# A recurrence's tables: readout weights and guard on GpSimd instead of VectorE, and a doubling in three operations

## The chip, the cores and the metric

The kernel runs on one core of one Trainium2 chip. A core has engines that run side by side, each with its own list of instructions: TensorE (matrix products, PE in the rows), VectorE (DVE), ScalarE (ACT), GpSimd (POOL) and SyncE (SP), which here only issues transfers. They wait for each other by counters (semaphores). The metric is the time of one execution on the device in microseconds, the median of several runs.

## The reference

It is a sandwich of three layers over 4096 tokens with 256 features: an expert layer, a linear recurrence over the whole sequence, and the same expert layer again, each added to its input.

```python
x = L0_attn_u                                   # (1, 4096, 256)
x = x + 0.5 * ffn(layernorm(x), Wr, W1, b1, W2, b2)
x = x + ssm(layernorm(x), A_real, A_imag, B, C)
x = x + 0.5 * ffn(layernorm(x), Wr, W1, b1, W2, b2)

# ffn: 8 experts, each token goes to the one of its largest score
probs = softmax(x @ Wr); e = argmax(probs); p = max(probs)
out = p * (gelu(x @ W1[e] + b1[e]) @ W2[e] + b2[e])

# ssm: 128 complex states, real input and output
a = A_real + 1j * A_imag;  denom = 1 - dt / 2 * a
a_disc = (1 + dt / 2 * a) / denom;  B_disc = sqrt(dt) * B / denom[:, None]
h_t = a_disc * h_{t-1} + B_disc @ u_t;  y_t = (C @ h_t).real
```

## The kernel before, in words

**Stages.** Loading, statistics, routing and the splitting of the expert weights into two half-precision parts take the first 85 us. The first expert layer runs to about 306 us, the recurrence (eight chunks of 512 tokens) to about 385, the second expert layer to the end.

**The expert layer.** The tokens are sorted by expert into 39 tiles of at most 128 rows (`NT`). Thirty-two are full; of the seven narrow ones (16 to 112 rows), four (in places 18, 23, 28 and 33 of the order) lie between the full ones and three come last. The loop over tiles `q` is written out by hand for each engine, in a software pipeline:

- GpSimd, per tile: wait for `result(q)` (counter `o`), issue the scatter of the finished rows (line 427), then the two gathers of tile q + 6 (line 421: the rows, and the records with the token's norm and weight).
- ScalarE, per tile: normalise the gathered rows, scale the turned rows to the first half-precision part, and GELU (line 620) in eight pieces of 128 columns.
- TensorE, per tile: turn tile q + 2, first product of tile q + 1 (line 1337, 48 matmuls), second product of tile q (lines 1359 to 1361). The first product of a tile waits for `split_x` of that tile; the second for `split_h`.
- VectorE, per tile: `split_x(q + 2)` (line 1006, the second half-precision part of the input, from PSUM), `split_h(q + 1)` (lines 1018 and 1021, twice: both parts of GELU's result), `result(q)` (lines 1035 and 1038, and in the first layer bn_stats and bn_aggr, lines 1041 and 1042), and in the first layer a piece of table work, `tables_after(q)`.

`result(q)` writes one of two buffers, and so waits for the scatter of tile q - 2 to have landed.

**The tables.** The recurrence is run in a frame that turns with each state, so that a real-valued scan does the work. It needs, for the 512 steps of a chunk, the turns (`turn`: cosine and sine of n times the angle), the readout weights (`back`), a guard that moves weights near zero away from it, and the reciprocal of the product of the two weights. They have 128 x 512 columns in two parts, and are made in pieces after `result(q)`: doublings of `turn` after tiles 2 to 14 (from tile 8 on in pieces of 64 columns), the weights after tiles 15 to 22 (two instructions each on 128 columns), the guard after tiles 23 to 30 (three instructions each on 128 columns), product and reciprocal of 64 columns after tiles 31 to 37, and a last piece with the rest of the tables after the loop. `link` makes an engine wait for its own instruction's end.

After the layer SyncE waits for all scatters, reloads x (eight transfers), GpSimd computes the norm's factors of the first chunk, and VectorE goes on in `turn_by_rates` (line 1174).

## Time and profile before

| what | value |
|---|---|
| median of 3 runs | 613.46 us (611.41 to 613.84) |
| profiled execution | 611.62 us, of which the span from first to last instruction is 609.8 |
| TensorE busy | 550.4 us (90% of the span) |
| VectorE busy | 479.6 us (79%) |
| ScalarE busy | 410.0 us (67%) |
| GpSimd busy | 287.5 us (47%) |
| granted TensorE clock, mean | 0.987 |

Busy time is that of an engine's own instructions, and a share of the whole span is an average over the stages. Starts are microseconds from the start of the span. What an engine waited for is inferred from the counters' events. Matmuls overlap, and their ends are modelled. An operation of GpSimd counts from when it begins to read to when its writes are done, so what it waits for within it is in its duration.

### The profile page before, as it was taken

The page shows a single profiled execution, that of the slowest core. Times are in us where ns is not written, and L with a number is a line of the kernel's source. Part 1 is how long each engine was busy: PE and PEld are TensorE (multiplying, and loading weights), DVE is VectorE, ACT ScalarE, POOL GpSimd, SP SyncE. Part 2 cuts the span into 40 slices and gives each one's busy share as a digit, 9 for nine tenths or more (in the row PEclk, how much of TensorE's full clock was granted, in tenths as well). Part 3 has the DMA queues.
Part 4 walks back from the last instruction along what each step waited for, and adds up shares of the span by engine and source line. Part 5 has one row for each costly group of instructions (what it writes and reads, how often), then busy time and mean ns, then how long its engine had stood idle before and what let it go on. Part 6 is the DMA issues. An engine that isn't in the chain of part 4 may idle for free.

```text
span 609.8 us, 18742 instructions
## 1 busy us (share of the span) xinstructions
PE 550.4 (90%) x6518; PEld 505.6 (83%) x6518; DVE 479.6 (79%) x1082; ACT 410.0 (67%) x966; POOL 287.5 (47%) x325
## 2 busy tenths in 40 slices
PE   5993148999999999999989998699999999999996
PEld 5993047999998999998976776599999999999996
DVE  5778997999999889898978988466667666666674
ACT  3888978767766676766615862386766777766763
POOL 0024165565454555654136243556555555545532
PEclk9999999999999999999999996899999999999999
DMA  7999102111121111111053223212111111111110
GB/s 248 369 370 378 38 26 97 54 55 46 46 53 47 37 53 45 53 38 45 23 191 125 75 99 107 60 44 57 47 45 53 54 48 44 46 46 46 52 28 16
DMA packets 34874, 51.95 MB, mean 85 GB/s; under 512 B 6747, under 2 KB 27933, under 8 KB 34528
## 3 DMA queue, kind: packets, MB, share of 16 engines
q1 hardware_dynamic: 24800, 31.93, 15.3%
q0 software_dynamic: 9984, 18.83, 11.3%
q8 instruction: 56, 0.92, 0.6%
q14 instruction: 34, 0.28, 0.2%
HBM read 37.98 MB, written 14.59 MB: 86 GB/s over the span
## 4 chain that ended last, share of the span: by engine, by line
PE 71%; DVE 10%; issue 6%; POOL 4%; DMA 3%; ACT 3%; DVEq 1%; SPq 0%; ACTq 0%; POOLq 0%
PE banks L1337 27%; PE banks L1359 10%; PE banks L1361 9%; PE banks L1360 9%; PE banks L1267 4%; PE banks L1312 2%; PE banks L1239 2%; PE banks L1446 2%; DVE weights_arena L1018 2%; DVE weights_arena L1021 1%; PE banks L1414 1%; PE banks L1429 1%; POOL weights_arena L421 1%; DMA recf<-records,sorti 1%; DVE weights_arena L1038 1%
## 5 line engine op out<-in xcount | busy, mean ns | idle before, releaser
L620 ACT ACTIVATE weights_arena<-banks,b1t,inv 128x128 f32<-128x128 f32 (+7 forms) x624 | 220.6, 459 | 34.4 <-PE banks L1337 34.3
L1337 PE MATMUL banks<-weights_arena 128*128 128x128 f16 (+7 forms) x3744 | 207.0, 214 | 3.0 <-DVE weights_arena L1006 2.2
L1337 PEld LDWEIGHTS banks<-weights_arena 128*128 x3744 | 199.3, 98 | 6.6 <-issue 5.5
L1359 PE MATMUL banks<-weights_arena 128*128 (+7 forms) x624 | 170.2, 273 | 0.5 <-DVE weights_arena L1021 0.3
L1361 PE MATMUL banks<-weights_arena 128*128 (+7 forms) x624 | 170.1, 273 | 0.0
L1360 PE MATMUL banks<-weights_arena 128*128 (+7 forms) x624 | 170.1, 273 | 0.0
L1018 DVE TENSOR_SCALAR weights_arena<-weights_arena,hscale 128x512 f16<-128x512 f32 (+5 forms) x156 | 74.7, 479 | 57.1 <-ACT weights_arena L620 56.2
L1021 DVE SCALAR_TENSOR_TENSOR weights_arena<-weights_arena,hscale 128x512 f16<-128x512 f32 (+5 forms) x156 | 109.8, 704 | 5.6
L601 ACT ACTIVATE weights_arena<-banks,xscale 128x256 f16<-128x256 f32 (+7 forms) x78 | 35.7, 457 | 89.8 <-PE banks L1312 89.8
L421 POOL DMA_INDIRECT recf<-records,sorti x78 | 76.5, 981 | 24.6 <-issue 23.5
L427 POOL DMA_INDIRECT x_after_ffn<-weights_arena,sorti x39 | 39.7, 1019 | 80.8 <-DVE weights_arena L1042 74.2
L427 POOL DMA_INDIRECT out<-weights_arena,sorti x39 | 39.5, 1013 | 78.2 <-DVE weights_arena L1038 70.8
L1359 PEld LDWEIGHTS banks<-weights_arena 128*128 128x128 f16 (+7 forms) x624 | 62.3, 100 | 7.3 <-issue 1.1
L1361 PEld LDWEIGHTS banks<-weights_arena 128*128 128x128 f16 (+7 forms) x624 | 62.4, 100 | 6.4
L1360 PEld LDWEIGHTS banks<-weights_arena 128*128 128x128 f16 (+7 forms) x624 | 62.4, 100 | 5.6
L421 POOL DMA_INDIRECT weights_arena<-L_attn_u,sorti x39 | 45.7, 1171 | 29.0 <-DVE sorti L984 17.4
L585 ACT ACTIVATE weights_arena<-weights_arena,recf 128x256 f32<-128x256 f32 (+7 forms) x78 | 46.1, 591 | 9.6 <-DMA recf<-records,sorti 9.5
L1035 DVE SCALAR_TENSOR_TENSOR weights_arena<-banks,inv,weights_arena 128x256 f32<-128x256 f32 (+7 forms) x78 | 37.7, 483 | 14.3 <-issue 5.6
L421 POOL DMA_INDIRECT weights_arena<-x_after_ssm,sorti x39 | 40.5, 1038 | 15.1 <-issue 11.6
L1006 DVE SCALAR_TENSOR_TENSOR weights_arena<-banks,xscale,weights_arena 128x256 f16<-128x256 f32 (+7 forms) x78 | 35.6, 457 | 12.5 <-ACT weights_arena L601 7.8
L1038 DVE SCALAR_TENSOR_TENSOR weights_arena<-weights_arena,recf 128x256 f32<-128x256 f32 (+7 forms) x78 | 37.8, 484 | 2.8
L729 DVE SCALAR_TENSOR_TENSOR weights_arena<-weights_arena,wscale 128x2048 f16<-128x2048 f32 x16 | 37.2, 2342 | 2.7 <-ACT weights_arena L516 2.7
(238 smaller groups left out, 648.7 us busy)
## 6 DMA issues: line engine op xcount, KB each, us to landing
weights_arena<-L_ffn_W SPq DMA_DIRECT2D x16, 1024.0 KB, 12.6
weights_arena<-x_after_ffn SPq DMA_DIRECT2D x8, 516.0 KB, 7.3
weights_arena<-L_attn_u SPq DMA_DIRECT2D x8, 512.0 KB, 11.1
x_after_ssm<-weights_arena SPq DMA_DIRECT2D x8, 512.0 KB, 2.9
weights_arena<-L_ffn_b SPq DMA_DIRECT2D x2, 1024.0 KB, 5.2
recf<-records,sorti POOLq DMA_INDIRECT x78, 2.5
weights_arena<-L_attn_u,sorti POOLq DMA_INDIRECT x39, 3.2
x_after_ffn<-weights_arena,sorti POOLq DMA_INDIRECT x39, 2.5
```

The lines of the kernel that those rows point to most:

```text
L421: pool.indirect_dma_start(to, None, source, bass.IndirectOffsetOnAxis(ap=sorti[:, slot(q), index:index + 1].bitcast(U32), axis=0)).then_in ...
L427: pool.indirect_dma_start(dst, bass.IndirectOffsetOnAxis(ap=sorti[:, slot(q), 2:3].bitcast(U32), axis=0), og[q % 2] if ph == 1 else og[q % ...
L585: act.activation(xng[q % 2][0:w], xg[q % RING][0:w], ACT.Identity, bias=recf[0:w, q % RING, 0:1], scale=recf[0:w, q % RING, 1:2]).then_inc ...
L620: last = act.activation(hb[q % 2][:, f, 0:width(q)], src, ACT.Gelu, bias=b1t[:, bass.ds(e * FC + f, 1)], scale=inv1[:, bass.ds(e, 1)])
L1018: dve.tensor_scalar(hs[q % 2][:, 0, f, of], hb[q % 2][:, f, of], sc, None, ALU.mult) \
L1021: dve.scalar_tensor_tensor(hs[q % 2][:, 1, f, of], hb[q % 2][:, f, of], sc, hs[q % 2][:, 0, f, of], ALU.mult, ALU.subtract).then_inc(s["hs ...
L1035: dve.scalar_tensor_tensor(o, acc, i2, b2b[0:w, bass.ds(e * D, D)], ALU.mult, ALU.add) \
L1038: last = dve.scalar_tensor_tensor(o, o, recf[0:w, q % RING, 2:3], xg[q % RING][0:w], ALU.mult, ALU.add)
L1337: last = pe.matmul(acc[:, f * P:f * P + n_cols], weights[wpart * DC + d], xts[q % 2][:, xpart, d, 0:n_cols], start=(n == 0), stop=(n == 5))
L1359: pe.matmul(acc, hs[q % 2][:, 0, f, of], high, start=(f == 0), stop=False)
L1360: pe.matmul(acc, hs[q % 2][:, 0, f, of], low, start=False, stop=False)
L1361: last = pe.matmul(acc, hs[q % 2][:, 1, f, of], high, start=False, stop=(f == FC - 1))
```

## The change

Readout weights, guard and the product of the weights leave VectorE. GpSimd makes them in 13 operations on 128 x 512 columns each (`weights_after`), one behind the scatter and the two gathers of each of tiles 15 to 27; the guard and the weights are taken apart into operations with two inputs or with one input and scalars. A counter tells GpSimd that the turns are made (`turns_made`, at tile 14), another tells VectorE that the product is (`weights_made`); VectorE waits for it from tile 29 on, and keeps only the reciprocals, all eight within the loop (tiles 29 to 36). A doubling takes three instructions in place of four: the two products with the sine are one instruction over both parts. Four counters of the start are merged into two (`pool_made`, `dve_made`).

```diff
--- before.py
+++ after.py
@@ -375,15 +375,15 @@
...
-            pool.wait_ge(iota_done, 3)
-            pool.wait_ge(rho_in, 1)
-            pool.tensor_tensor(ev[:, 13:14], ev[:, 12:13], mhalf[:, 0:1], ALU.pow).then_inc(rho_out, 1)
+            pool.wait_ge(pool_made, 3)
+            pool.wait_ge(dve_made, 3)
+            pool.tensor_tensor(ev[:, 13:14], ev[:, 12:13], mhalf[:, 0:1], ALU.pow).then_inc(pool_made, 1)
@@ -401,6 +401,34 @@
                 chain.link(pool.tensor_scalar(vid[:, NJ:NTE], over_experts[:, NJ:NTE, 0], -1.0, None, ALU.add))
                 pool.tensor_scalar(vid_h, vid, BIG / P, None, ALU.add).then_inc(S[ph]["vids"], 1)
 
+            def weights_after(q):
+
+                link = chain.link
+                if q == 15:
+                    pool.wait_ge(turns_made, 1)
+                    link(pool.tensor_scalar(aa[:, 0, :], turn[:, 0, :], ev[:, 15:16], None, ALU.mult))
+                elif q == 16:
+                    link(pool.tensor_scalar(aa[:, 1, :], turn[:, 1, :], ev[:, 15:16], None, ALU.mult))
+                elif q == 17:
+                    link(pool.tensor_scalar(inverse[:, 0, :], turn[:, 0, :], ev[:, 14:15], None, ALU.mult))
+                elif q == 18:
+                    link(pool.tensor_scalar(inverse[:, 1, :], turn[:, 1, :], ev[:, 14:15], None, ALU.mult))
+                elif q == 19:
+                    link(pool.tensor_tensor(back[:, 0, :], inverse[:, 0, :], aa[:, 1, :], ALU.subtract))
+                elif q == 20:
+                    link(pool.tensor_tensor(back[:, 1, :], inverse[:, 1, :], aa[:, 0, :], ALU.add))
+                elif q in (21, 22):
+                    weight = back[:, q - 21, :]
+                    link(pool.tensor_tensor(aa[:, q - 21, :], weight, weight, ALU.mult))
+                elif q in (23, 24):
+                    near = aa[:, q - 23, :]
+                    link(pool.tensor_scalar(near, near, NEAR_ZERO ** 2, STAND_IN, ALU.is_lt, ALU.mult))
+                elif q in (25, 26):
+                    weight = back[:, q - 25, :]
+                    link(pool.tensor_tensor(weight, weight, aa[:, q - 25, :], ALU.add))
+                elif q == 27:
+                    pool.tensor_tensor(aa[:, 0, :], back[:, 0, :], back[:, 1, :], ALU.mult).then_inc(weights_made, 1)
+
             def ffn(ph, src, dst):
                 s = S[ph]
                 table = src
@@ -434,6 +462,8 @@
                     scatter(q)
                     if q + RING < NT:
                         fetch(q + RING)
+                    if ph == 1:
+                        weights_after(q)
 
             tile_slots(1)
             ffn(1, u, x1_dram)
@@ -681,15 +711,15 @@
...
-            dve.tensor_scalar(ident[:], iota_r[:], part[:], None, ALU.is_equal).then_inc(const_done, 1)
+            dve.tensor_scalar(ident[:], iota_r[:], part[:], None, ALU.is_equal).then_inc(dve_made, 1)
@@ -764,9 +794,9 @@
-                dve.scalar_tensor_tensor(col(12), col(11), col(11), col(16), ALU.mult, ALU.add).then_inc(rho_in, 1)
-                dve.wait_ge(rho_in, 1)
-                dve.wait_ge(rho_out, 1)
+                dve.scalar_tensor_tensor(col(12), col(11), col(11), col(16), ALU.mult, ALU.add).then_inc(dve_made, 1)
+                dve.wait_ge(dve_made, 3)
+                dve.wait_ge(pool_made, 5)
@@ -774,33 +804,15 @@
             def double(n, begin=0, end=None):
 
                 end = n if end is None else end
-                c0, s0 = turn[:, 0, begin:end], turn[:, 1, begin:end]
+                of, to = slice(begin, end), slice(n + begin, n + end)
                 cn, sn = turn[:, 0, n - 1:n], turn[:, 1, n - 1:n]
-                dve.tensor_scalar(back[:, 0, begin:end], s0, sn, None, ALU.mult)
-                link(dve.tensor_scalar(back[:, 1, begin:end], c0, sn, None, ALU.mult))
-                dve.scalar_tensor_tensor(turn[:, 0, n + begin:n + end], c0, cn, back[:, 0, begin:end], ALU.mult, ALU.subtract)
-                link(dve.scalar_tensor_tensor(turn[:, 1, n + begin:n + end], s0, cn, back[:, 1, begin:end], ALU.mult, ALU.add))
-
-            def readout(part, begin, end):
+                link(dve.tensor_scalar(back[:, :, of], turn[:, :, of], sn, None, ALU.mult))
+                dve.scalar_tensor_tensor(turn[:, 0, to], turn[:, 0, of], cn, back[:, 1, of], ALU.mult, ALU.subtract)
+                link(dve.scalar_tensor_tensor(turn[:, 1, to], turn[:, 1, of], cn, back[:, 0, of], ALU.mult, ALU.add))
+
+            def inverse_of_both(begin, end):
 
                 of = slice(begin, end)
-                col_a, col_b, how = (0, 1, ALU.subtract) if part == 0 else (1, 0, ALU.add)
-                tmp = aa[:, part, of]
-                link(dve.tensor_scalar(tmp, turn[:, col_b, of], col(15), None, ALU.mult))
-                link(dve.scalar_tensor_tensor(back[:, part, of], turn[:, col_a, of], col(14), tmp, ALU.mult, how))
-
-            def away_from_zero(part, begin, end):
-
-                of = slice(begin, end)
-                tmp, weight = aa[:, part, of], back[:, part, of]
-                link(dve.tensor_tensor(tmp, weight, weight, ALU.mult))
-                link(dve.tensor_scalar(tmp, tmp, NEAR_ZERO ** 2, None, ALU.is_lt))
-                link(dve.scalar_tensor_tensor(weight, tmp, STAND_IN, weight, ALU.mult, ALU.add))
-
-            def inverse_of_both(begin, end):
-
-                of = slice(begin, end)
-                link(dve.tensor_tensor(aa[:, 0, of], back[:, 0, of], back[:, 1, of], ALU.mult))
                 link(dve.reciprocal(aa[:, 0, of], aa[:, 0, of]))
 
             def inverses(part):
@@ -826,7 +838,6 @@
-                piece = CH // 4 * ((q - 15) // 2)
@@ -835,13 +846,11 @@
                     double(CH // 4, CH // 8 * (q - 9), CH // 8 * (q - 8))
                 elif 11 <= q < 15:
                     double(CH // 2, CH // 8 * (q - 11), CH // 8 * (q - 10))
-                elif 15 <= q < 23:
-                    readout((q - 15) % 2, piece, piece + CH // 4)
-                elif 23 <= q < 31:
-                    piece = CH // 4 * ((q - 23) // 2)
-                    away_from_zero((q - 23) % 2, piece, piece + CH // 4)
-                elif 31 <= q < NT - 1:
-                    inverse_of_both(CH // 8 * (q - 31), CH // 8 * (q - 30))
+                    if q == 14:
+                        dve.sem_inc(turns_made, 1)
+                elif 29 <= q < 37:
+                    dve.wait_ge(weights_made, 1)
+                    inverse_of_both(CH // 8 * (q - 29), CH // 8 * (q - 28))
 
             def bounds_up():
 
@@ -1065,7 +1074,6 @@
                 if ph == 1:
                     dve.memset(state[:], 0.0)
                     dve.memset(all_ones, 1.0)
-                    inverse_of_both(CH // 8 * (NT - 32), CH)
                     inverses(0)
                     inverses(1)
                     carries()
```

## Rows read from the trace of the kernel before

**Rows 1.** Busy time by stretch, first expert layer: length; PE, PEld, DVE, ACT, POOL busy.

```profile
168.38:191.70 23.32, 22.59 (x299) 20.78 (x297) 21.44 (x52) 15.39 (x40) 11.46 (x12) 1.00 0.18 47
191.70:272.67 80.97, 80.35 (x1111) 75.12 (x1111) 72.32 (x175) 56.10 (x150) 46.68 (x47) 1.00 0.18 46
272.67:293.95 21.28, 20.73 (x299) 18.90 (x296) 19.03 (x46) 14.52 (x40) 9.95 (x10) 1.00 0.17 46
```

**Rows 2.** Busy time by stretch, second expert layer.

```profile
470.72:492.72 22.00, 22.00 (x298) 20.91 (x296) 15.12 (x29) 15.38 (x40) 12.07 (x13) 1.00 0.18 51
492.72:572.72 80.00, 80.00 (x1113) 75.24 (x1111) 54.37 (x106) 56.05 (x150) 45.16 (x46) 1.00 0.18 47
572.72:593.27 20.55, 20.55 (x299) 18.94 (x296) 14.12 (x29) 14.53 (x40) 8.33 (x9) 1.00 0.16 39
```

**Rows 3.** Waits of TensorE, 157.35 to 293.95: total us, times, longest.

```profile
PE banks L1337 <- DVE weights_arena L1006: 1.2, 2, 0.6
```

**Rows 4.** Timeline of VectorE at both layers' ends: start, length, line, [idle before].

```profile
305.96 0.47 DVE L1035 SCALAR_TENSOR_TENSOR weights_arena<-banks,inv,weights_arena 16x256 f32<-16x256 f32 x1 [0.38 <-PE banks L1361]
...
313.57 0.21 DVE L825 TENSOR_SCALAR back<-back,rho 128x1 f32<-128x1 f32 x1
315.83 0.31 DVE L1174 TENSOR_SCALAR weights_arena<-ident,rs 128x128 f32<-128x128 f32 x1 [2.05 <-POOL sd L449]
...
604.84 0.47 DVE L1035 SCALAR_TENSOR_TENSOR weights_arena<-banks,inv,weights_arena 16x256 f32<-16x256 f32 x1 [1.72 <-PE banks L1361]
```

**Rows 5.** Timeline of VectorE, a tile with a 64-wide doubling.

```profile
160.37 0.18 DVE L1042 BATCH_NORM_AGGREGATE weights_arena<-stats 128x2 f32<-128x6 f32 x1
160.47 0.22 DVE L779 TENSOR_SCALAR back<-turn 128x64 f32<-128x64 f32 x1
160.60 0.25 DVE L780 TENSOR_SCALAR back<-turn 128x64 f32<-128x64 f32 x1
...
161.91 0.72 DVE L1018 TENSOR_SCALAR weights_arena<-weights_arena,hscale 128x512 f16<-128x512 f32 x1
```

**Rows 6.** Groups of VectorE by line, 104 to 316 us: busy, mean ns, idle before.

```profile
L804 DVE RECIPROCAL weights_arena<-weights_arena 128x64 f32<-128x64 f32 x8 | 4.4, 553 | 0.3
...
L790 DVE SCALAR_TENSOR_TENSOR back<-turn,ev,weights_arena 128x128 f32<-128x128 f32 x8 | 2.8, 352 | 0.3
...
L789 DVE TENSOR_SCALAR weights_arena<-turn,ev 128x128 f32<-128x128 f32 x8 | 2.0, 254 | 0.0
```

**Rows 7.** Timeline of GpSimd, transfers of the same tile.

```profile
161.37 1.01 POOL L427 DMA_INDIRECT x_after_ffn<-weights_arena,sorti  x1 [2.38 <-DVE weights_arena L1042]
...
163.96 0.94 POOL L421 DMA_INDIRECT recf<-records,sorti  x1 [0.30 <-issue]
```

**Rows 8.** Timeline of VectorE, a tile with a 32-wide doubling.

```profile
144.48 0.48 DVE L1018 TENSOR_SCALAR weights_arena<-weights_arena,hscale 128x512 f16<-128x512 f32 x1
```

**Rows 9.** Timeline of VectorE, tiles without table work.

```profile
105.15 0.48 DVE L1035 SCALAR_TENSOR_TENSOR weights_arena<-banks,inv,weights_arena 128x256 f32<-128x256 f32 x1
...
106.65 0.18 DVE L1042 BATCH_NORM_AGGREGATE weights_arena<-stats 128x2 f32<-128x6 f32 x1
...
107.16 0.48 DVE L1018 TENSOR_SCALAR weights_arena<-weights_arena,hscale 128x512 f16<-128x512 f32 x1
...
109.80 0.48 DVE L1035 SCALAR_TENSOR_TENSOR weights_arena<-banks,inv,weights_arena 128x256 f32<-128x256 f32 x1
```

**Rows 10.** Groups by line and shape of GpSimd, 54 to 64 us.

```profile
L398 POOL TENSOR_TENSOR weights_arena<-weights_arena 128x160 f32<-128x160 f32 x1 | 0.5, 523 | 0.1
L398 POOL TENSOR_TENSOR weights_arena<-weights_arena 128x80 f32<-128x80 f32 x1 | 0.3, 323 | 0.1
```

**Rows 11.** Timeline of VectorE and GpSimd at 60 us.

```profile
60.10 2.33 DVE L729 SCALAR_TENSOR_TENSOR weights_arena<-weights_arena,wscale 128x2048 f16<-128x2048 f32 x1
...
60.27 2.33 POOL L402 TENSOR_SCALAR weights_arena<-weights_arena 128x40 f16<-128x40 f32 x1
```

**Rows 12.** DMA issues of the first layer's scatter: median us to landing.

```profile
x_after_ffn<-weights_arena,sorti POOLq DMA_INDIRECT x39, 2.5
```

22 lines of the change are left out of this document (11 added, 11 removed).

## The prediction

> **What bounds the kernel now.** I set the two expert layers beside each other, because they run the same tiles over the same expert weights and only the first carries the table work on VectorE. Cut at the starts of the same first products (tiles 12, 14, 18, 33 and 37), the view of busy time by stretch gives, for tiles 14 to 18, 18 to 33 and 33 to 37, lengths of 23.32, 80.97 and 21.28 us in the first layer [rows 1] and 22.00, 80.00 and 20.55 in the second [rows 2]. In the second layer TensorE is busy for the whole of each. In the first it is idle for part of each, and VectorE is busy for 21.44 of 23.32, 72.32 of 80.97 and 19.03 of 21.28. So TensorE bounds the second layer and VectorE, at these places, the first; the list of waits names `split_x` (line 1006) as what the first product waited for [rows 3]. The differences, 1.32 + 0.97 + 0.73 = 3.02 us, are what VectorE costs between tiles 14 and 37. From the start of tile 37's first product to the last tile's `result` it is 305.96 - 293.95 = 12.01 in the first layer and 604.84 - 593.27 = 11.57 in the second [rows 1, 2, 4]: 0.44 more. **3.46 us is the ceiling** of what relief of VectorE can bring here.
>
> Behind the layer nothing else catches the end: VectorE's own tail of table work ends at 313.57 + 0.21 = 313.78, and its next work starts at 315.83 [rows 4], having waited for GpSimd, which waited for the reload of x. That cover is 2.05 us. The last scatter, the reload and all that follows hang on the last `result`, so an earlier end of the layer is passed on whole; the tail loses one small piece of work itself (line 803 and 804 for the last 64 columns), under cover.
>
> **The change, part by part.**
>
> *Doublings in three operations (tiles 2 to 14).* Before, lines 779 and 780 start at 160.47 and 160.60, so the first costs 0.13 us of VectorE's time, and from line 1042 to line 1018 it takes 161.91 - 160.37 = 1.54 [rows 5]. The new first instruction works on 2 x 64 columns at once. No row has that form; the nearest are 128 x 64 at 0.25 (line 780) [rows 5] and 128 x 128 at 0.254 (line 789) [rows 6]. So it costs nothing to 0.05 more than line 780, and I take 0.03: a saving of 0.10 a tile, 1.3 over 13 tiles. There is a second effect. Line 1018 took 0.72 while a scatter was issued (161.37 to 162.38) [rows 5, 7] and 0.48 in the tile with half as wide a doubling [rows 8]; starting 0.10 earlier it may get ahead of it, which is worth 0 to 0.24 a tile. A tile without tables takes VectorE 109.80 - 105.15 = 4.65 us, of which 0.51 lies between lines 1042 and 1018 [rows 9]; TensorE takes 22.00 / 4 = 5.50 [rows 2]. With a 64-wide doubling VectorE needs 4.65 + (1.54 - 0.51) + 0.24 = 5.92, 0.42 too much for each of seven tiles (8 to 14), 2.9 in all; 1.32 of it reached TensorE, so a lead of some 1.6 took up the rest. With 0.10 less a tile 7 x 0.32 = 2.2 stands against a lead of 1.6 + 0.6 (tiles 2 to 7) = 2.2; with 0.34 less, 0.6. I take 0.2 as left over: **1.1 us gained of 1.32**.
>
> *Weights, guard and product leave VectorE (tiles 15 to 30).* The weights were two instructions a tile (0.254 and 0.352 us [rows 6]), the guard three, the product one before each reciprocal. Now tiles 15 to 28 have no table work, VectorE needs 4.65 of 5.50, and its lead grows by up to 0.85 a tile. Tiles 29 to 36 keep the reciprocal at 0.553 [rows 6], so 5.3 of 5.50. The narrow tiles (18, 23, 28 and 33), where TensorE takes some 0.8 less (15 x 5.50 - 80.00 = 2.5 for three of them [rows 2]) and VectorE still runs `result` at full length, were what VectorE paid for in the last two stretches; a lead of 2 us covers each. **0.9 of 0.97, 0.7 of 0.73, 0.4 of 0.44.**
>
> *Thirteen GpSimd operations, one behind each tile's transfers (tiles 15 to 27).* What GpSimd does for a tile now runs from 161.37 to 163.96 + 0.94 = 164.90, 3.53 us [rows 7]. No row shows 128 x 512 on GpSimd. The largest is 128 x 160 with two inputs at 523 ns, and 128 x 80 took 323 [rows 10]: 2.5 ns a column, so 0.523 + 352 x 0.0025 = 1.40 us. The bounds are 0.52 (no dearer than the smaller one) and 1.67 (in proportion). For the forms with one input and a scalar, the only row of any width is 40 columns in 2.33 us, and that one began at 60.27, right behind a VectorE instruction that began at 60.10 and took 2.33, and ended 0.17 after it [rows 11]: a wait, not work. I give them the same 1.40. Then a tile is 3.53 + 0.30 + 1.40 = 5.23 of 5.50: it fits, with little over. Queued behind each operation (the link waits for its end) are the next scatter and two gathers. The gathers are issued six tiles ahead. A scatter starts 161.37 - 160.55 = 0.82 after `result` ends [rows 5, 7] and lands 2.5 later [rows 12]; `result` of two tiles later waits for it, 1.7 (106.65 + 0.18 - 105.15 [rows 9]) before that tile's own end, so the slack is 11.0 - 1.7 - 0.82 - 2.5 = 6.0 us. The work is hidden as long as GpSimd runs less than that behind. At tile 29 VectorE waits for the last of it, issued at tile 27: a tile and more of slack.
>
> *Semaphores.* The merged counters are waited on in the same order by the same engines; two new waits replace two old ones. Nothing is queued that was not before: zero.
>
> *Does GpSimd hold up VectorE?* GpSimd waits there for a two-input VectorE instruction [rows 11], and line 1018 at 0.72 instead of 0.48 [rows 5, 8] shows the reverse. When VectorE has its lead, the operation starts 0.3 after the second gather, 164.90 + 0.30 - 160.55 = 4.65 after a `result` ends, which with a period of 5.50 is 0.5 before the next `result`'s bn_stats: mostly over work that reads PSUM or a single input. A collision is then paid from an idle 0.85 a tile. I take nothing, with a bound of 1.40 a tile. The Trainium skill, SBUF — State Buffer, section Who interferes with whom, says that a VectorE instruction with two SBUF inputs contends with a GpSimd one that reads SBUF, and that the later one is blocked for the whole of the earlier; the wait of 2.33 us agrees, and by that rule the reverse could cost whole operations, which is the first rival below.
>
> **Sum.** 1.1 + 0.9 + 0.7 + 0.4 = 3.1 us off the profiled execution's 611.62, so 608.5. The median of the runs is 1.84 above that execution (613.46), so the predicted median is 613.46 - 3.1 = **610.4**. 0.5% is 3.07 us, about what this measurement can tell from no change: the forecast lies on that line.
>
> **Rivals.**
> - *The port takes half of it back.* If each operation holds VectorE for about half its length, 0.7 a tile, VectorE needs 5.35 of 5.50 in tiles 15 to 27: no loss on wide tiles, but no lead for the narrow ones, so the 0.9 is not gained and 0.1 of the rest goes: 613.46 - 2.1 = 611.4. For the whole 1.40, 6.05 of 5.50 costs 13 x 0.55 = 7.2 less a lead of some 2, 5.2 in place of the 0.97, and the time is 613.46 - 2.2 + 4.2 = 615.5. For it: the two rows above. Against it: of the lines of a tile only 1021 and 1038 read two SBUF tensors, and only 1018 is slowed in the rows; together they are about half of VectorE's time.
> - *Slower: GpSimd becomes the bound.* If an operation takes d, GpSimd runs 3.83 + d a tile; above d = 1.67 it falls behind, and above 1.67 + 6.0 / 13 = 2.1 the scatters come too late for `result`, which stalls. At d = 3.0 that is 13 x 1.33 - 6.0 = 11.3 us: 613.46 - 3.1 + 11.3 = 621.7. For it: the instruction of 40 columns that took 2.33 [rows 11]. Against it: the slope of the two rows that waited for nothing [rows 10].
> - *The change does not do what it says.* The lead does not build because GpSimd and VectorE fall into step (5.23 and 4.65 plus what they cost each other), and the doublings' collision with the scatter stays at 0.72: only some 0.7 comes from the doublings: 612.8.
>
> **Numbers.** Forecast 0.62 (between a gain of 2.5 and the ceiling: 610.0 to 611.0); half taken back 0.20; no effect 0.10; GpSimd the bound 0.08. The line of 0.5% cuts the forecast's own range, and the runs of one kernel spread by 0.4%, so of 0.62 about 0.43 falls under 3.07 us faster, the rest and the second and third cases within 0.5%, and 0.09 above. The range reaches from the lowest run less the ceiling, 611.41 - 3.46 = 608.0, to 613.3, which takes in the two cases without much gain and leaves out the whole-length lock and the GpSimd bound.
>
> **What would show it.** Right: the first layer's stretches near 22.0, 80.0 and 20.6; TensorE busy throughout; line 789 to 798 gone from VectorE; the new GpSimd rows at 0.5 to 1.7 us; the first wait of line 1018 for GELU instead of none. The doubling's saving shows as the distance from line 1042 to line 1018 at 1.2 to 1.45 instead of 1.54. Wrong: GpSimd rows over 2 us, scatters later and later from tile 15 to 27, `result` waiting for a scatter; or lines 1018, 1021 and 1038 stretched to over 1 us in those tiles.

## The result, and the profile after

The changed kernel took 615.66 us in the median of 20 runs (613.41 to 617.39), the kernel before 611.85 in 20 runs beside it (609.21 to 615.65): a ratio of 1.0066, 95% interval 1.0050 to 1.0081. It is slower: the whole interval lies at 0.5% or more. 610.4 in a range of 608.0 to 613.3 was forecast. Of all the runs below, one execution stood far apart (`e3_pow`: 701.45 us at a mean granted clock of 0.77, the others at 0.92 and more) and is left out there.

Busy time by stretch of the changed kernel, first expert layer, cut at the first products of tiles 14, 18, 33 and 37 (answers to [rows 1]; after the length come the busy times of PE, PEld, DVE, ACT and POOL):

```profile
166.84:188.83 21.99, 21.99 (x298) 20.91 (x296) 19.96 (x46) 15.38 (x40) 12.08 (x13) 1.00 0.19 48
188.83:274.64 85.81, 81.95 (x1112) 74.73 (x1110) 74.12 (x136) 55.32 (x150) 65.78 (x58) 1.00 0.16 42
274.64:296.33 21.69, 20.73 (x299) 18.90 (x296) 19.25 (x43) 14.57 (x40) 10.33 (x11) 1.00 0.19 45
```

Tiles 14 to 18 gained the whole 1.32 us, but tiles 18 to 33, forecast at 80.1, took 85.81 against 80.97. Finer cuts put the loss at tiles 23 to 28 (28.59 us, before 26.72) and 28 to 33 (30.43, before 26.69); tiles 18 to 23 stand at 26.78. The last result comes at

```profile
307.91 0.47 DVE L1044 SCALAR_TENSOR_TENSOR weights_arena<-banks,inv,weights_arena 16x256 f32<-16x256 f32 x1 [0.36 <-PE banks L1369]
```

so the end takes 307.91 - 296.33 = 11.58 against 12.01 [rows 1, 4]. From tile 14 to this result it is 141.07 us, where it was 305.96 - 168.38 = 137.58: **3.49 us lost in the place where 3.1 were to be gained**. Of the rest of the span, 1.5 us were gained up to tile 14, 0.5 lost between the layers and 0.7 at the start of the second layer. The first and the last are within what executions of the same code differ by: the changed kernel and three of the kernels below whose code is the same there (the late wait, the held and the later products) reach tile 14 between 166.84 and 169.23 us, and take 214.4 to 215.4 us from the second layer's first product to the end.

What did go as forecast: a tile with a 64-wide doubling, on VectorE (answers to [rows 5]; L1027 is the former L1018):

```profile
158.11 0.18 DVE L1051 BATCH_NORM_AGGREGATE weights_arena<-stats 128x2 f32<-128x6 f32 x1
158.21 0.25 DVE L809 TENSOR_SCALAR back<-turn 128x128 f32<-128x128 f32 x1
...
159.52 0.48 DVE L1027 TENSOR_SCALAR weights_arena<-weights_arena,hscale 128x512 f16<-128x512 f32 x1
```

The distance is 1.41 in place of 1.54, and line 1027 is back at 0.48 from 0.72. It does not get ahead of the scatter for that; the scatter of this tile is

```profile
159.10 1.01 POOL L455 DMA_INDIRECT x_after_ffn<-weights_arena,sorti  x1 [2.09 <-DVE weights_arena L1051]
```

and line 1027 starts 0.42 into it, where line 1018 had started 161.91 - 161.37 = 0.54 into it [rows 5, 7]. In the profiles of before, after and the doublings alone (125 to 186 us, 512 columns) this line took 0.47 to 0.49 wherever it started up to 0.45 into a scatter, and 0.72 in all seven places where it started 0.54 or 0.55 into one.

What did not go as forecast, first on GpSimd, from one scatter to the next with an operation between them (answers to [rows 7]):

```profile
186.92 1.13 POOL L455 DMA_INDIRECT x_after_ffn<-weights_arena,sorti  x1 [2.37 <-DVE weights_arena L1051]
188.35 0.97 POOL L449 DMA_INDIRECT weights_arena<-L_attn_u,sorti  x1 [0.30 <-issue]
189.63 0.95 POOL L449 DMA_INDIRECT recf<-records,sorti  x1 [0.31 <-issue]
190.63 1.79 POOL L409 TENSOR_SCALAR weights_arena<-turn,ev 128x512 f32<-128x512 f32 x1
193.23 1.17 POOL L455 DMA_INDIRECT x_after_ffn<-weights_arena,sorti  x1 [0.82 <-POOL weights_arena L409]
```

One round (from one scatter to the next) takes 193.23 - 186.92 = 6.31 us; TensorE needs 5.50 a tile. The operation took 1.79, and the scatter behind it began only 0.82 after its end. GpSimd's groups by line, 160 to 297 us, show two prices:

```profile
L425 POOL TENSOR_SCALAR weights_arena<-weights_arena 128x512 f32<-128x512 f32 x2 | 4.3, 2142 | 0.2
L428 POOL TENSOR_TENSOR back<-back,weights_arena 128x512 f32<-128x512 f32 x2 | 2.5, 1272 | 0.1
```

The six operations with one input took 1.78 to 2.27 us, the seven with two 1.05 to 1.28. The rounds take 6.3 to 6.7 us with one input and 5.4 to 5.9 with two. So GpSimd falls behind from tile 15 on, and everything in its queue with it. The waits of ScalarE and of TensorE, 155 to 297 us (total, times, longest; before, ScalarE waited for no transfer there, and TensorE's row is [rows 3]):

```profile
ACT weights_arena L615 <- DMA recf<-records,sorti: 22.8, 11, 3.8
```

```profile
PE banks L1345 <- DVE weights_arena L1015: 3.2, 5, 1.0
PE banks L1367 <- DVE weights_arena L1030: 0.6, 1, 0.6
```

Line 615 is ScalarE's norm, which needs the gathered rows of three tiles ahead; it stands in ScalarE's order ahead of the next tile's GELU (line 650). The chain at 237 us, on ScalarE and then on VectorE:

```profile
236.87 0.60 ACT L615 ACTIVATE weights_arena<-weights_arena,recf 48x256 f32<-48x256 f32 x1 [3.77 <-DMA recf<-records,sorti]
237.38 2.86 ACT L650 ACTIVATE weights_arena<-banks,b1t,inv 128x128 f32<-128x128 f32 x8
```

```profile
239.05 0.49 DVE L1027 TENSOR_SCALAR weights_arena<-weights_arena,hscale 128x512 f16<-128x512 f32 x1 [1.78 <-ACT weights_arena L650]
```

A late gather, a late norm, a late GELU, an idle VectorE, and with it the lead is gone. The second thing that differs is the length of VectorE's own instructions when GpSimd runs an operation beside them:

```profile
227.61 2.02 DVE L1030 SCALAR_TENSOR_TENSOR weights_arena<-weights_arena,hscale 128x512 f16<-128x512 f32 x1
```

```profile
228.02 1.05 POOL L422 TENSOR_TENSOR weights_arena<-back 128x512 f32<-128x512 f32 x1
```

Line 1030 reads two SBUF tensors and takes 0.75 alone; here, and at four other places between 221 and 264 us, it took 1.97 to 2.25. Two theories stood: the **queue** (GpSimd's longer round delays gathers and scatters) and the **port** (GpSimd's reads hold VectorE).

### The profile page after: what moved, and what is told of

Read it like the earlier page. It is cut to its first block, busy times and chain, and to the rows that moved or that the text cites. A ratio compares the mean times of both kernels' runs of the same rounds, so it can differ in the third digit from the quotient of the medians.

```text
span 613.0 us, 18692 instructions
## 1 busy us (share of the span) xinstructions
PE 549.0 (90%) x6518; PEld 503.4 (82%) x6518; DVE 477.3 (78%) x1021; ACT 408.8 (67%) x966; POOL 310.6 (51%) x338
## 4 chain that ended last, share of the span: by engine, by line
PE 62%; DVE 9%; POOL 8%; issue 7%; DMA 7%; SPq 3%; ACT 2%; DVEq 0%; ACTq 0%; POOLq 0%
PE banks L1345 25%; PE banks L1367 9%; PE banks L1369 9%; PE banks L1368 9%; DMA recf<-records,sorti 2%; PE banks L1320 2%; POOL weights_arena L449 2%; DMA weights_arena<-L_attn_u 2%; PE banks L1275 2%; DVE weights_arena L1030 1%; SPq L327 1%; PE banks L1422 1%; SPq L310 1%; PE banks L1437 1%; POOL recf L449 1%
## 5 line engine op out<-in xcount | busy, mean ns | idle before, releaser
L1027 DVE TENSOR_SCALAR weights_arena<-weights_arena,hscale 128x512 f16<-128x512 f32 (+5 forms) x156 | 74.6, 478 | 64.0 <-ACT weights_arena L650 63.4
L1030 DVE SCALAR_TENSOR_TENSOR weights_arena<-weights_arena,hscale 128x512 f16<-128x512 f32 (+5 forms) x156 | 118.0, 756 | 5.6
L449 POOL DMA_INDIRECT recf<-records,sorti x78 | 78.9, 1011 | 24.9 <-issue 23.5
L1047 DVE SCALAR_TENSOR_TENSOR weights_arena<-weights_arena,recf 128x256 f32<-128x256 f32 (+7 forms) x78 | 40.3, 516 | 2.8
```

Of the source, the lines that this page charges most:

```text
L449: pool.indirect_dma_start(to, None, source, bass.IndirectOffsetOnAxis(ap=sorti[:, slot(q), index:index + 1].bitcast(U32), axis=0)).then_in ...
L1027: dve.tensor_scalar(hs[q % 2][:, 0, f, of], hb[q % 2][:, f, of], sc, None, ALU.mult) \
L1030: dve.scalar_tensor_tensor(hs[q % 2][:, 1, f, of], hb[q % 2][:, f, of], sc, hs[q % 2][:, 0, f, of], ALU.mult, ALU.subtract).then_inc(s["hs ...
L1047: last = dve.scalar_tensor_tensor(o, o, recf[0:w, q % RING, 2:3], xg[q % RING][0:w], ALU.mult, ALU.add)
```

## The experiments

In all of them "stretches" are the lengths of tiles 14 to 18, 18 to 23, 23 to 28, 28 to 33, 33 to 37 and the end, from the same cuts. Before they are 23.31, 27.57, 26.72, 26.69, 21.28 and 12.01; after 22.00, 26.78, 28.59, 30.43, 21.69 and 11.58. Ratios are to the kernel before, run beside each on the same chip; runs without a ratio had one execution.

**Doublings alone** (`e1_doublings`): the kernel before with the three-operation `double`; weights, guard and product stay on VectorE.

```diff
-                dve.tensor_scalar(back[:, 0, begin:end], s0, sn, None, ALU.mult)
-                link(dve.tensor_scalar(back[:, 1, begin:end], c0, sn, None, ALU.mult))
+                link(dve.tensor_scalar(back[:, :, of], turn[:, :, of], sn, None, ALU.mult))
...
```

> Only the doublings in three operations; weights, guard and product stay on VectorE in their pieces. Queue theory (GpSimd's tile became longer than TensorE's, gathers come late) and port theory (GpSimd's operations hold VectorE's two-input instructions) both put the whole loss on the GpSimd operations: then this is 1.3 to 1.8 us faster than before, first-layer stretches 14 to 18 at 22.0 to 22.2 and 18 to 33 at 80.5 to 81. If the loss came from the doublings or from the rest of the change, it is 1 us or more slower.

Measured: 610.94 us, ratio 0.9998 (0.9972 to 1.0024); stretches 22.00, 26.78, 26.72, 27.02, 21.29, 12.37. The layer is 1.41 us shorter (2.10 gained in tiles 14 to 23, 0.70 lost again from 28 on), and the total does not show it (below, "where the gain went").

**Nothing on GpSimd** (`e2_no_gpsimd`): the changed kernel without its 13 operations; VectorE makes the weights behind the loop, and its reciprocals in tiles 29 to 36 work on other numbers, so that its load in the loop stays.

```diff
-                    if ph == 1:
-                        weights_after(q)
...
...
+                    for part_of in range(2):
+                        readout(part_of, 0, CH)
+                    for part_of in range(2):
+                        away_from_zero(part_of, 0, CH)
+                    link(dve.tensor_tensor(aa[:, 0, :], back[:, 0, :], back[:, 1, :], ALU.mult))
+                    inverse_of_both(0, CH)
                     inverses(0)
```

> The changed kernel with no weights, guard or product in the loop, neither on GpSimd nor on VectorE: VectorE makes them in full width after the loop, and within it takes reciprocals of other numbers of the same size, which are not used. Both theories: first-layer stretches as in the second layer, 22.0, 80.0 and 20.6, and no wait of ScalarE's norm for a gather; the time as a whole is some 5 us above before, as 11 us of VectorE's work now lie behind the layer, of which 2 are covered. If the loss had another cause than the GpSimd operations, stretches 18 to 33 stay at 85 and 33 to 37 at 21.7.

Measured: 616.65, ratio 1.0105 (1.0053 to 1.0157), since the work behind the loop adds 97.17 - 89.59 = 7.6 us between the layers; stretches 22.00, 26.78, 26.72, 26.49, 20.76, 11.98. Without GpSimd's operations the layer's loss is gone whole: they are its cause, not the order of VectorE's remaining work. (The waits on the two new counters go with them; in the changed kernel neither engine stood idle at one, and the next run has neither and loses as much.)

**A queue without a port** (`e3_pow`): as the last, but behind each of tiles 15 to 27 GpSimd raises 7 columns to a power, with the same wait behind it; that reads nearly nothing.

```diff
+                if 15 <= q < 28:
+                    link(pool.tensor_tensor(var1[:, 0:7], iota_r[:, 1:8], mhalf[:, 0:7], ALU.pow))
```

> As the one before, with 13 GpSimd operations in the same places that read only 7 columns (a power, estimated at 1.5 us from 8 columns in 1.66 and 4 in 1.04), so that GpSimd is as long as in the changed kernel but reads next to nothing. Queue theory: stretch 18 to 33 at 83 or more, ScalarE's norm waits 10 us or more for gathers. Port theory: 80.0 to 80.5, and the second instruction of split_h stays at 0.75.

Measured: 623.65 (three executions), ratio 1.0223 (1.0159 to 1.0287); stretches 22.00, 26.78, 27.27, 31.34, 22.69, 11.58. GpSimd, then ScalarE's wait:

```profile
208.81 1.64 POOL L408 TENSOR_TENSOR var<-iota_r,mhalf 128x7 f32<-128x7 f32 x1
211.28 1.04 POOL L433 DMA_INDIRECT x_after_ffn<-weights_arena,sorti  x1 [0.83 <-POOL var L408]
```

```profile
ACT weights_arena L593 <- DMA recf<-records,sorti: 23.6, 11, 3.4
```

The powers take 1.56 us in the mean and the next scatter again waits 0.83: rounds of 6.0 to 6.2 us, 79.6 for all 13, where those of the real operations took 78.7. VectorE's two-input lines stand at their means of before (0.70 and 0.48 us, 186 to 275 us), so the port has no part. That alone costs as much in the layer (141.68 us from tile 14 to the last result, after 141.07) as the real operations do. The queue is sufficient.

**More gathers ahead** (`e4_ring8`): the changed kernel with `RING = 8` for 6, two more buffers of gathered rows; the reload shares the counters of the first load to make room.

```diff
-RING = 6
+RING = 8
...
```

> The changed kernel with gathers eight tiles ahead instead of six (and the reload's counters shared with the first load's, to have counters for it). Queue theory: gathers are in time again, stretch 18 to 33 back to 80.0 to 80.8, time 2.5 to 3.4 us below before. Port theory: the stretch stays over 83, the time 1 us or more above before. If both act, in between: 81 to 83.

Measured: 614.55, ratio 1.0064 (1.0038 to 1.0090); stretches 22.00, 26.78, 26.72, 31.24, 21.57, 11.57. The norm waits for no gather any more, but the rounds are as long as in the changed kernel, and now the scatters are too late. VectorE's waits, 225 to 280 us, and two rows of its timeline:

```profile
DVE weights_arena L1044 <- DMA x_after_ffn<-weights_arena,sorti: 5.9, 3, 3.4
```

```profile
251.88 0.48 DVE L1044 SCALAR_TENSOR_TENSOR weights_arena<-banks,inv,weights_arena 128x256 f32<-128x256 f32 x1 [3.41 <-DMA x_after_ffn<-weights_arena,sorti]
252.40 1.49 DVE L1047 SCALAR_TENSOR_TENSOR weights_arena<-weights_arena,recf 128x256 f32<-128x256 f32 x1
```

`result` may not overwrite its buffer until the scatter of two tiles earlier has landed. One late transfer took the place of another: the backlog, not the depth, is the trouble. Line 1047 at 1.49 for 0.48 shows the port beside it: it took 1.05 in the mean of 15 tiles (186 to 275 us), so this run does not part the two.

**The late wait** (`e5_deferred`): the changed kernel with one thing moved. GpSimd waits for an operation's end just before its next operation, no longer right behind it, so that the scatter between does not wait.

```diff
-                link = chain.link
+                def link(instruction):
+                    instruction.then_inc(pool_chain, 1)
+                    chain.n += 1
+                if 15 < q < 28:
+                    pool.wait_ge(pool_chain, chain.n)
```

> The changed kernel, but GpSimd waits for an operation of the weights just before the next one, not right behind it, so the scatter can follow in 0.3 us and not in 0.82. Queue theory (GpSimd's own 6.3 to 6.6 us a tile against TensorE's 5.5 delay scatters and gathers): a tile with a two-input operation falls to about 5.4 and one with a one-input operation to about 6.1, so tiles 23 to 28 take about 27.0 us and 28 to 33 about 27.0, where the changed kernel's profile has 28.59 and 30.43, and the time is 611 to 613. Port theory (a two-input operation of GpSimd holds VectorE's two-input operations from 0.75 to 2.0 us): the stretches stay 1 to 2 us longer than those of the kernel before, 18 to 33 in all about 84, and the time is 614 to 616.

Measured: 610.94, ratio 0.9985 (0.9953 to 1.0016); stretches 22.00, 26.78, 26.72, 26.50, 20.77, 11.58. GpSimd, and busy time from tile 18 to 28 in two stretches:

```profile
192.29 1.79 POOL L415 TENSOR_SCALAR weights_arena<-turn,ev 128x512 f32<-128x512 f32 x1
194.26 1.05 POOL L461 DMA_INDIRECT x_after_ffn<-weights_arena,sorti  x1 [0.18 <-issue]
```

```profile
190.50:217.28 26.78, 26.78 (x372) 25.43 (x370) 22.45 (x46) 18.82 (x50) 22.66 (x21) 1.00 0.17 44
217.28:244.00 26.72, 26.72 (x373) 25.07 (x370) 22.12 (x46) 18.67 (x50) 22.39 (x21) 1.00 0.18 46
```

The scatter follows after 0.18 us in place of 0.82; the operations are the same and take as long. TensorE is busy throughout, and the layer is 134.35 us from tile 14 to the last result: 6.72 less than after, 3.23 less than before. **The 0.64 us of hand-over (from an operation's end to the next transfer), behind 12 of the 13 operations, decided the sign of the layer's change.** The whole time is below the changed kernel's (the intervals are apart) and can't be told from that of before. With another timing the operations also held VectorE less (line 1036 took 0.69 us in the mean of 186 to 275 us, its counterpart 1030 in the changed kernel 0.97); that the loss needs no port is shown by the powers, not by this run.

**Late wait and more gathers** (`e6_both`): both edits.

```diff
-RING = 6
+RING = 8
...
+                if 15 < q < 28:
+                    pool.wait_ge(pool_chain, chain.n)
```

> The late wait and eight gathers ahead in place of six. Queue theory: nothing waits for a gather or a scatter any longer, tiles 23 to 28 take 26.7 us and 28 to 33 at most 26.8, and the time is 610 to 611. Port theory: as with the late wait alone, 28 to 33 at 28 to 30 and the time 613 to 615.

Measured: 610.66, ratio 0.9993 (0.9963 to 1.0022); stretches 22.00, 26.78, 27.75, 27.33, 21.24, 11.59. No one waits for a transfer, yet the layer is 2.3 us longer than with the late wait alone: TensorE waited 2.0 us for `split_x` (line 1021 of this kernel), and line 1053 (the former 1047) took 0.735 us in the mean of 186 to 275 us for 0.510 there. That is the port.

**Port against queue at one load** (`e9_two_inputs`, `e10_pow_deferred`): both edits, and in place of the weights equal operations that take GpSimd alike: 13 two-input products of 128x512 (1.28 us) in the one, 12 powers of 5 columns (1.26 us) in the other, which has none behind tile 27. The weights are made by VectorE behind the loop, as above.

```diff
+                if 15 <= q < 27:
+                    link(pool.tensor_tensor(aa[:, 0, :], turn[:, 0, :], turn[:, 1, :], ALU.mult))
...
+                    link(pool.tensor_tensor(var1[:, 0:5], iota_r[:, 1:6], mhalf[:, 0:5], ALU.pow))
```

> Late wait, eight gathers ahead, and in place of the weights 13 equal two-input operations of 128x512 behind tiles 15 to 27 (the weights are made by VectorE behind the loop, which adds some 7 us there). Port with no queue: 1.28 us each keeps GpSimd at 5.4 us a tile. Queue theory: tiles 18 to 23, 23 to 28 and 28 to 33 stand at 26.8, 26.7 and 26.5 us. Port theory: each operation takes 1.2 to 1.5 us from VectorE, which has about 0.5 us free in a tile, so each of the stretches 18 to 23 and 23 to 28 is 2 to 4 us longer.

> The same, but with 13 powers over 5 columns, which take about as long on GpSimd (1.1 to 1.3 us) and read nearly nothing (the weights are made by VectorE behind the loop). Queue with no port. Both theories: GpSimd at 5.4 us a tile keeps up, and the three stretches stand at 26.8, 26.7 and 26.5 us. If they are longer than that, GpSimd's time in the queue costs even under 5.5 us a tile, and the two-input kernel's stretches must be read against this one's.

Measured, one execution each: 617.0 and 619.39. Stretches of the products: 22.00, 27.69, 26.72, 26.49, 20.55, 11.58; of the powers: 22.00, 26.78, 26.72, 26.49, 20.77, 11.58. VectorE's groups by line, 186 to 275 us, with the products and then with the powers:

```profile
L1051 DVE SCALAR_TENSOR_TENSOR weights_arena<-weights_arena,recf 128x256 f32<-128x256 f32 (+3 forms) x16 | 12.6, 790 | 0.6
```

```profile
L1051 DVE SCALAR_TENSOR_TENSOR weights_arena<-weights_arena,recf 128x256 f32<-128x256 f32 (+3 forms) x17 | 8.2, 484 | 0.6
```

Over 16 tiles line 1051 lost 16 x 0.306 = 4.9 us and line 1031 (0.628 for 0.489) about 4.7, and of these 9.6 us only 0.9 reached TensorE: VectorE had the lead to pay it. The port theory's 2 to 4 us a stretch are refuted for this place of the operations; the powers show that rounds of 5.0 to 5.7 us cost nothing.

**The last products held back** (`e12_held_inverses`): the late wait, and VectorE begins its two products behind the last tile when GpSimd says that the last scatter has been issued. The reason for it, a longer last scatter, is told in the next section ("so an earlier end of the layer is passed on whole").

```diff
+                if ph == 1:
+                    pool.sem_inc(weights_made, 1)
...
+                    dve.wait_ge(weights_made, 2)
                     inverses(0)
```

> The kernel with the late wait, and VectorE begins the two products behind the last tile (L820 in the changed kernel) only when GpSimd has issued the last scatter. In the changed kernel and the three built on it the last scatter took 1.49 us while such a product ran on VectorE at its start, in the kernel before 0.98, and the reload of the rows began 5.14 to 5.22 us behind the last result in place of 4.63. Theory that VectorE's two-input operation holds the scatter: the scatter is back at 0.98 and the reload at 4.6, the stage between the layers is 0.5 us shorter, and the time about 608 to 610. Rival, that the late start has another cause (the last tile's own landing, or GpSimd's queue): the reload stays at 5.1 to 5.2. In both the first layer's stretches stay at 22.00, 26.78, 26.72, 26.50, 20.77 and 11.58.

Measured: 610.28, ratio 0.9996 (0.9969 to 1.0023); stretches 22.00, 26.78, 26.72, 27.66, 21.22, 11.58. The signal overtook the scatter: VectorE's product began 0.17 us ahead of it instead of 0.70, and the scatter took

```profile
305.37 1.37 POOL L461 DMA_INDIRECT x_after_ffn<-weights_arena,sorti  x1 [0.97 <-DVE weights_arena L1059]
```

with the reload at 5.02. So this run did not take the product away from the scatter's start; the next one did. It told something else: up to tile 37 its loop is that of the late wait alone, and yet 28 to 33 and 33 to 37 took 1.6 us more, with TensorE waiting 1.5 us for `split_x`. The port's price changes from one execution to another, with where GpSimd's operation falls in VectorE's tile: here `result` of one narrow tile was held for 2.04 us (line 1055, for 0.48) beside an operation of 1.05.

**The last products later** (`e14_later_products`): the late wait, with the last two pieces of the reciprocals moved behind the last tile, ahead of the two products.

```diff
-                elif 29 <= q < 37:
+                elif 29 <= q < 35:
...
+                    inverse_of_both(CH // 8 * 6, CH // 8 * 7)
+                    inverse_of_both(CH // 8 * 7, CH)
                     inverses(0)
```

> The late wait, and the last two pieces of 64 reciprocals are made behind the last tile, ahead of the two products, in place of tiles 35 and 36: some 1.2 us more work of one input on VectorE there. So the first product begins about 0.5 us behind the last scatter's start and not 0.7 ahead of it. Theory that a two-input operation of VectorE at the scatter's start lengthens it: the last scatter takes 0.98 us in place of 1.49 and the reload begins 4.6 us behind the last result in place of 5.2, though VectorE has more to do there. Rival, that the longer scatter comes from GpSimd's operations in the loop or from the shorter end: 1.4 to 1.5 and 5.1 to 5.2 as before. The end, 11.58, gains nothing or loses up to 0.4 by neither.

Measured, one execution: 612.74; stretches 22.00, 26.78, 26.72, 26.50, 21.07, 11.58. The last scatter on GpSimd, and VectorE's first product:

```profile
306.30 0.97 POOL L461 DMA_INDIRECT x_after_ffn<-weights_arena,sorti  x1 [1.03 <-DVE weights_arena L1057]
```

```profile
306.71 1.42 DVE L826 TENSOR_TENSOR weights_arena<-back,weights_arena 128x512 f32<-128x512 f32 x2
```

The reload begins 4.79 us behind the last result, 0.43 earlier than with the late wait alone, though VectorE has more to do behind the last tile. The theory held for the scatter: with the product starting 0.41 us behind its start it takes 0.97, with one running at its start 1.49. For the reload 4.6 was forecast.

**ScalarE in place of GpSimd** (`e13_scalar_held`): the doublings in three operations; no table work on GpSimd. ScalarE makes four operations of 512 columns, VectorE the rest, with the last products held as in `e12_held_inverses`.

```diff
+                    if ph == 1 and q in (16, 17):
+                        act.wait_ge(turns_made, 1)
+                        act.activation(aa[:, q - 16, :], turn[:, 17 - q, :], ACT.Copy, scale=ev[:, 15:16]).then_inc(weights_made, 1)
+                    if ph == 1 and q in (21, 23):
+                        part = (q - 21) // 2
+                        act.wait_ge(turns_made, part + 2)
+                        act.activation(aa[:, part, :], back[:, part, :], ACT.Square).then_inc(weights_made, 1)
...
```

> ScalarE in place of GpSimd: it makes the two multiplications by the readout's small part behind its norm of tiles 19 and 20 and the two squares behind those of 24 and 26; VectorE makes the weights with one operation of 256 columns in each of four tiles, tests the squares and adds in pieces of 128 in eight tiles, and the product and reciprocals in pieces of 64 in tiles 30 to 37; the last products are held as in the other kernel of this call. If the work itself was never the trouble but only where it was put (GpSimd's queue and port), the stretches stand at 22.00, 26.78, 26.72, 26.6, 20.9 and 11.6 and the time is that of the other kernel, 608 to 610. If ScalarE's longest wait, for TensorE, is no room (its GELU and norm come late), the stretches of 18 to 28 are 0.5 to 1 us longer.

Measured: **609.40, ratio 0.9963 (0.9942 to 0.9984)**; stretches 22.00, 26.78, 26.72, 26.50, 20.67, 12.05. ScalarE's groups by line, 160 to 297 us:

```profile
L631 ACT ACTIVATE weights_arena<-turn,ev 128x512 f32<-128x512 f32 x2 | 1.4, 711 | 0.0
L635 ACT ACTIVATE weights_arena<-back 128x512 f32<-128x512 f32 x2 | 1.2, 617 | 0.0
```

Four operations of 0.6 to 0.7 us, once in a tile at most, on an engine that waited 31 us for TensorE in these tiles, and TensorE waits for nobody. Its interval lies below 1, and below the changed kernel's.

**The same without the hold** (`e15_scalar_later`; the edit is against the run above): the last 64 columns of product and reciprocal stand behind the last tile, as in the kernel before.

```diff
-                elif 30 <= q < NT - 1:
+                elif 30 <= q < NT - 2:
...
-                    dve.wait_ge(weights_made, 5)
+                    inverse_of_both(CH // 8 * 7, CH)
                     inverses(0)
```

> ScalarE in place of GpSimd, without the hold; the last piece of product and reciprocals (64 columns) stands behind the last tile, as in the kernel before, so VectorE's products begin 0.07 us behind the last scatter's start. Theory that they hold the scatter only when they run at its start: the scatter takes 0.98 and the reload begins at 4.63, 0.4 earlier than with the hold (5.04); the time is 608.5 to 609.5, or that of the kernel with the hold, 609.4, if the clock of the chunks covers it. Rival: the scatter stays at 1.4 and the reload at 5.0. The stretches stand at 22.00, 26.78, 26.72, 26.50, 20.7 and 11.6 to 12.05 in both.

Measured: **609.50, ratio 0.9976 (0.9954 to 0.9999)**; stretches 22.00, 26.78, 26.72, 26.50, 20.66, 12.00; last scatter 0.98 us, reload at 4.64 as forecast. So a second kernel with this work on ScalarE is faster than before, if only just by its interval; whether it or the one with the hold is the better can't be told.

## Why the prediction was wrong

*Doublings: right.* 1.1 of 1.32 us was forecast for tiles 14 to 18; all of it came, in the changed kernel and with the doublings alone. The 0.24 a tile of line 1018 came too, though not as the prediction had it: the line starts 0.42 into the scatter in place of 0.54 and is not slowed there, without getting ahead of it.

*Weights, guard and product leave VectorE: right in size, where GpSimd does not spoil it.* 0.9, 0.7 and 0.4 were forecast; with the late wait 26.78 + 26.72 + 26.50 = 80.00 for 80.97, 20.77 for 21.28 and 11.58 for 12.01 give 0.97, 0.51 and 0.43. With the doublings that is 3.23 against a sum of 3.1 and a ceiling of 3.46.

*"Then a tile is 3.53 + 0.30 + 1.40 = 5.23 of 5.50: it fits": this step failed, in two of its terms.* The 1.40 was 1.05 to 1.28 for two inputs, but 1.78 to 2.27 for one, of which the prediction said "I give them the same 1.40", over a row of 40 columns in 2.33 us that it had put down to a wait. That reading was right, but the trace of before had more: the same line runs again at 380.87 us and takes 0.71 there (into float16), where line 398 with two inputs takes 0.26 for 40 columns. And the 0.30 is the gap between two transfers, which wait for nothing. Behind an operation that GpSimd itself waits for, the gap is 0.82; the prediction had that number, for the way from `result` to its scatter, and did not use it for GpSimd's wait on itself, though it wrote that "the link waits for its end". So a round was 6.3 to 6.7 us with one input and 5.4 to 5.9 with two. The powers show that rounds of 6.0 to 6.2 are enough for the whole loss, the late wait that 0.64 us less is enough to lose nothing: the one-input operations at their real price still make rounds of 5.5 to 6.1 us there, which costs the lead a little and TensorE nothing.

*"The gathers are issued six tiles ahead" was taken for ample.* The slack that was worked out, 6.0 us, is the scatter's. Before, the gather of tile 12 is issued, and its norm starts, at

```profile
141.40 0.94 POOL L421 DMA_INDIRECT recf<-records,sorti  x1 [0.30 <-issue]
```

```profile
146.98 0.59 ACT L585 ACTIVATE weights_arena<-weights_arena,recf 128x256 f32<-128x256 f32 x1
```

With 2.3 us to landing (its median in 120 to 200 us), counted from the issue's start or its end, that leaves 2.3 to 3.3 us, which three or four rounds of 0.8 too much use up. The norm is early by three tiles, and a gather waits for `result` of six tiles earlier. With eight ahead this wait went, and the scatter's 6.0 us were used up in its turn.

*The rivals.* "GpSimd becomes the bound", at 0.08, is what happened: its mechanism, scatters and gathers too late, and its place. Its threshold, d above 1.67, left out the hand-over; with 0.82 for 0.30 it is 1.15, which all but two of the 13 operations pass. "The port takes half of it back" happened too, between 0 and 2.3 us as the phase falls, but it was not needed for the loss. The Trainium skill, SBUF — State Buffer, section Who interferes with whom, says that a VectorE instruction with two SBUF inputs contends with a GpSimd one that reads SBUF, and that the ports they share are an exclusive lock. The trace agrees in size: line 1030 took 2.02 us for 0.75 beside an operation of 1.05. By the records line 1030 had started 0.41 us ahead of the operation and was held all the same, so which of the two is held can't be read from their starts. That the rival's price for whole operations, 615.5, stands next to the measured 615.66 is luck: it put the loss on the port, and the powers lose as much without one. "I take nothing" stood on a timing of GpSimd's operation that held only while GpSimd was on time, and that was misread: before, a `result` that ends at 106.83 runs its two-input line 1038 from 105.67 to 106.15 and bn_stats from 106.19, so 4.65 after the `result` ahead of it, at a period of 5.50, is 0.2 before bn_stats and not 0.5, within line 1038. It is this line that was held with both edits and with the products.

*"so an earlier end of the layer is passed on whole": not so.* Where the gain went with the late wait: 3.23 us shorter in the layer, and in the profiled execution 2.39 longer from the last `result` to the second layer's first product (91.98 for 89.59). Its parts, by the first table product of each of the scan's chunks: to the first 14.11 for 13.16 behind the last result; from there to the second 7.03 for 6.09, where VectorE waited 2.5 us for the reload of its rows (before 1.5); from the third to the fourth 7.49 for 6.17; the rest 0.82 less. That from third to fourth, beside the same one after, with the granted clock third from the end:

```profile
329.88:337.37 7.49, 7.26 (x30) 5.44 (x31) 5.96 (x10) 5.01 (x14) 1.40 (x6) 0.77 0.20 70
```

```profile
333.89:340.06 6.17, 6.17 (x38) 4.90 (x37) 5.89 (x10) 3.55 (x9) 1.40 (x6) 1.00 0.25 85
```

For part of it TensorE ran at 1.2 GHz, after the second chunk's step, in which it was busy for 4.93 of 7.03 us, and another of 5.80 in 5.89. Of the kernels that make the weights within the layer, the profiles of seven show such a stretch somewhere between 16 and 33 us behind the last `result` (the doublings alone, eight gathers ahead, the late wait, the held and the later products, both with ScalarE), those of before, after and of both edits none. From the last `result` to the second layer the three without it take 0, 0.51 and 0.81 us more than before's 89.59, the seven with it 1.29 to 3.62 more: most of what these versions did not gain lies there. Whether the earlier end of the layer brings the stretch on, one profile for each can't tell; this is open. A part that comes in every profile is the reload: it begins 4.63 us behind the last `result` before and with the doublings alone, 5.14 to 5.22 in the four kernels that make all the weights on GpSimd and leave the last products where the change put them. The last scatter, before and after:

```profile
308.37 0.98 POOL L427 DMA_INDIRECT x_after_ffn<-weights_arena,sorti  x1 [1.72 <-DVE weights_arena L1042]
```

```profile
310.33 1.49 POOL L455 DMA_INDIRECT x_after_ffn<-weights_arena,sorti  x1 [1.03 <-DVE weights_arena L1051]
```

Before, lines 803 and 804 for the last 64 columns stood ahead of VectorE's last products, which so began 0.07 us behind this scatter's start. The change took that piece into the loop, which the prediction counted as free ("under cover"), and now the products start at 309.63, 0.70 ahead of the scatter. With them later, or with that piece left in its place (`e15_scalar_later`), the scatter was back at 0.97 and 0.98: they hold it. So the 0.43 us gained at the end is lost again in 0.51 of scatter; in the changed kernel as much, 0.51 (90.10 for 89.59), is lost between the layers.

*The size.* The median rose by 615.66 - 611.85 = 3.8 us, the profiled layer by 3.49. The forecast also stood on a base of three runs, 613.46, which was 1.6 above the median of 20 beside the changed kernel; so the miss in the change is 3.8 + 3.1 = 6.9 us, not the 5.3 between the two times.

## What to carry to other kernels

Before work goes to an engine that has idle time, add up one whole round of its queue with every wait at its own price: a wait for one's own last instruction cost 0.82 us here, and 12 of them turned a gain into a loss. Put such a wait ahead of the next instruction that needs it, not behind the one that made it. For every transfer in that queue look up how long before its use it lands: the slack is that of the tightest user, and deeper buffers only pass a backlog on to the next one.

## What the runs showed of the hardware

- An elementwise operation with one input, a column of scalars or a constant, on 128x512 float32 took GpSimd 1.59 to 2.27 us, one with two input tensors 1.05 to 1.29: the one with less to read was the dearer.
- From the end of an operation of GpSimd, by way of a wait on its semaphore, to the start of its next indirect transfer it was 0.82 us (0.83 behind a power); with no wait between them 0.17 to 0.28 (behind powers 0.08 to 0.44).
- VectorE's two-input instruction of 512 columns took 1.97 to 2.25 us for 0.75, five times in the changed kernel, beside a two-input operation of GpSimd that takes 1.05 to 1.28; its two-input line of 256 columns took up to 2.29 for 0.48 (both edits). A slowed VectorE costs TensorE nothing as long as it has a lead: 9.6 us of it came out as 0.9 with the 13 products.
- The other way round, a two-input instruction of VectorE that runs when a scatter begins can lengthen it. In the fourteen profiles, 155 to 320 us, 67 scatters began while VectorE ran such instructions. Where these had begun at least 0.11 us before and ran on for at least 0.25, the scatter took 1.16 to 1.55 us (23 of them); the other 44 took 0.97 to 1.08.
